# Causal scores of a vision tower on one core: per-slot padding moved from the queries to the keys, with SBUF-to-SBUF DMAs, 392-column products and another order of the queues

## The reference

```python
h = _L0_tok_ref(x, ...)                                 # patches, norm, product, norm
h = h + _L0_attn_ref(_layernorm(h, axis=-1), ...)       # causal attention, 12 heads of 16
h = h + _L0_ffn_ref(_layernorm(h, axis=-1), ...)        # routed attention or mix, then MLP

# in _L0_attn_ref
q = q * scale
scores = jnp.einsum('bhid,bhjd->bhij', q, k)
scores = scores + jnp.einsum('bhid,jd->bhij', q, rel)
scores = jnp.where(causal, scores, -jnp.inf)
probs = jax.nn.softmax(scores, axis=-1)
y = jnp.einsum('bhij,bhjd->bhid', probs, v)
```

## Time and profile before

| | us |
|---|---|
| median of three runs | 7268.11 (7267.75 to 7270.31) |
| the profiled execution, first to last instruction (span) | 7259.2 |
| the profiled execution's own time outside the span | not noted; the median is 8.9 above the span |
| PE busy | 6605.1 |
| PEld busy | 5936.7 |
| DVE busy | 5383.8 |
| ACT busy | 3644.6 |
| POOL busy | 3111.4 |
| mean granted TensorE clock | 0.906 of 2.4 GHz |

### The profile page before, as it was taken

The page is one execution under the profiler, slowest core; times in us unless marked ns, Lnnn a source line. Parts: engine busy times, 40 slices in busy tenths (PEclk is TensorE's granted clock), DMA queues, the critical chain, the costliest instruction groups (busy, mean ns, idle before and its releaser), DMA issues.

```text
span 7259.2 us, 167273 instructions
## 1 busy us (share of the span) xinstructions
PE 6605.1 (91%) x56000; PEld 5936.7 (82%) x56000; DVE 5383.8 (74%) x15934; ACT 3644.6 (50%) x12160; POOL 3111.4 (43%) x4048
## 2 busy tenths in 40 slices
PE   4999999999999999999999999999999999999998
PEld 4888888888888888888888888888888888888887
DVE  3777777777777777777777777777777777777776
ACT  1545555554555455545545554555455455545554
POOL 4444444444444444444444444444444444444443
PEclk8889899999899998989989998999899999899998
DMA  4211121112111111211121111112111211121110
GB/s 46 29 22 23 22 29 22 23 22 29 22 23 26 25 23 22 27 23 23 22 29 22 23 25 25 23 22 28 23 23 22 29 22 23 22 29 22 23 24 8
DMA packets 228657, 175.83 MB, mean 24 GB/s; under 512 B 27785, under 2 KB 228126, under 8 KB 228630
## 3 DMA queue, kind: packets, MB, share of 16 engines
q1 hardware_dynamic: 218934, 173.46, 18.4%
q10 hardware_dynamic: 8336, 1.07, 0.2%
q0 software_dynamic: 1360, 0.96, 0.1%
HBM read 156.11 MB, written 19.27 MB: 24 GB/s over the span
## 4 chain that ended last, share of the span: by engine, by line
issue 34%; PE 20%; DVE 18%; POOL 15%; POOLq 9%; DVEq 3%; ACT 1%; ACTq 0%
PE bank L693 7%; POOL diag L502 6%; DVE qz L1109 5%; POOL rstd L487 4%; PE bank L645 4%; DVE negmax L1128 2%; DVE z L1062 2%; PE bank L681 2%; POOLq L556 2%; POOL h L557 2%; PE bank L781 2%; POOLq L486 2%; POOL res L565 2%; PE bank L792 2%; POOLq L582 2%
## 5 line engine op out<-in xcount | busy, mean ns | idle before, releaser
L1514 ACT ACTIVATE p<-bank,negmax 98x98 f32<-98x98 f32 (+1 forms) x3072 | 1132.3, 376 | 317.6 <-DVE negmax L1128 274.6
L714 PEld LDWEIGHTS bank<-diag,p 128*98 128x98 f32 x9216 | 1066.0, 202 | 157.1 <-issue 104.0
L714 PE MATMUL bank<-diag,p 128*98 128x98 f32 x9216 | 1175.1, 291 | 14.7 <-POOL diag L502 1.7
L1522 ACT COPY pT<-bank 98x392 f32<-98x392 f32 x768 | 374.7, 488 | 1542.2 <-PE bank L714 1542.1
L693 PE MATMUL bank<-tokw,x_sb 128*98 128x193 f32 x4096 | 924.3, 382 | 9.1 <-DVEq L1049 9.1
L502 POOL TENSOR_TENSOR diag<-ident,rden 98x588 f32<-98x588 f32 x512 | 608.4, 1199 | 648.2 <-DVE rden L1142 648.2
L693 PEld LDWEIGHTS bank<-tokw,x_sb 128*98 128x98 f32 x4096 | 825.0, 260 | 67.5 <-issue 29.2
L1128 DVE TENSOR_REDUCE negmax<-bank 98x1 f32<-98x196 f32 (+2 forms) x1536 | 626.1, 456 | 269.0 <-PE bank L681 268.7
L681 PE MATMUL bank<-qk_parts,qz 128*98 128x196 f32 (+1 forms) x6144 | 744.7, 265 | 0.0
L681 PEld LDWEIGHTS bank<-qk_parts,qz 128*98 128x98 f32 x6144 | 656.8, 166 | 11.4
L520 POOL TENSOR_TENSOR qz<-qk_parts,ones 32x588 fp32r<-32x588 f32 x256 | 301.2, 1176 | 721.8 <-DVE qk_parts L1099 701.5
(11 more groups left out here) (272 smaller groups left out, 14889.4 us busy)
## 6 DMA issues: line engine op xcount, KB each, us to landing
x_sb<-in_x SPq DMA_DIRECT2D x384, 196.0 KB, 4.8
x_sb<-in_x SPq DMA_DIRECT2D x384, 189.0 KB, 8.0
out<-out_row SPq DMA_DIRECT2D x128, 147.0 KB
x_store<-in_L_tok_W SPq DMA_DIRECT2D x6, 96.0 KB
diag<-in_L_ffn_W SPq DMA_DIRECT2D x1, 576.0 KB
gstore<-in_L_ffn_W SPq DMA_DIRECT2D x1, 384.0 KB
p<-in_L_attn_w_attn ACTq DMA_DIRECT2D x2, 96.0 KB
gstore<-in_L_ffn_W ACTq DMA_DIRECT2D x1, 192.0 KB
```

Source lines behind the costliest of these rows:

```text
L714: last = mm(bank[b][0:HT, HT * i:HT * i + HT], src, diag[:, h // 3, t, h % 3], start=True, stop=True)
L1514: sc.activation((p1 if t else p0)[0:HT, 3 * s + g], bank[b][0:HT, c0:c0 + (T if t else HT)], ACT.Exp, bias=negmax[:, s, t, g:g + 1], accum ...
L1522: sc.copy(pt_dst(name[0], int(name[1:])), bank[RING[name]][0:HT, 0:4 * HT]).then_inc(sem["pT_act"], 1)
```

## The change

- `wk` leads: k is projected before q, ScalarE copies `khi` and then loads its table and copies `qhi`, VectorE makes `klo` before `qparts`.
- `qz` and its four copies are gone. The queries' parts are used as they are. The keys get a padded tile `kz` of 128 x (2 parts, 4 slots, 3 groups, 196): for each image, SP issues four DMAs of 32 partitions x 2352 bytes for `khi`, and when `klo` is made four for that. They land behind the semaphores `khiz_in` and `kloz_in`, which S0 waits for.
- A score unit is now a group and a tile, nine in all: (g, t = 0) has four slots of 98 columns, (g, t = 1) is two units of two slots of 196. Each is a mask product and two products of 392 columns.
- `maxima` is one reduction in each unit, `inverse_sums` and `diagonals` are three in place of four (eight blocks in place of six).
- Order and banks: S8 after S7 on TensorE, A0 in bank 0, A1 in bank 3 (the embedding's), B0 ahead of A2; on VectorE `maxima(7)` ahead of `max2` and the patch variance, `maxima(3)` ahead of `inverse_sums(0)`; ScalarE copies A3 and VectorE A4.
- Room: `x_store` is gone, and the squares share `gstore`; `p2T` shares the scratch of the ranking; the raw embedding weights lie in `pT0`.

```diff
-RING = dict(S0=0, S1=1, S2=2, T0=3, S3=0, S4=1, S5=2, S6=0, S7=1, A0=2, A1=0, A2=3, B0=1, A3=2,
-            B1=0, A4=1, A5=3, B2=0)
+RING = dict(S0=0, S1=1, S2=2, T0=3, S3=0, S4=1, S5=2, S6=0, S7=1, S8=2, A0=0, A1=3, B0=1, A2=2,
+            A3=0, B1=1, A4=2, A5=3, B2=0)
-PT_ACT = ("A1", "B0", "B1", "A4", "A5", "B2")
+PT_ACT = ("A1", "B0", "A3", "B1", "A5", "B2")
 def s_unit(u):
-    s, second = divmod(u, 2)
-    if second:
-        return s, [(0, 1, 0), (1, 1, T)]
-    return s, [(2, 1, 0), (0, 0, T), (1, 0, T + HT), (2, 0, T + 2 * HT)]
+    g, part = divmod(u, 3)
+    if part:
+        return g, 1, range(2 * part - 2, 2 * part), T
+    return g, 0, range(4), HT
...
+            def place_keys(n):
+
+                for part, made, landed in ((0, "khi_sb", "khiz_in"), (1, "klo_sb", "kloz_in")):
+                    sp.wait_ge(sem[made], after(made, n))
+                    for s in range(4):
+                        at = slice(32 * s, 32 * s + 32)
+                        sp.dma_start(kz[at, part, s].bitcast(F32),
+                                     qk_parts[at, part].bitcast(F32)).then_inc(sem[landed], 16)
...
             with sp.Fori(0, B - 3) as j:
+                place_keys(j + 1)
                 prefetch(j + 2, j + 3)
                 store(j)
...
-                if front:
-
-                    for i in (2, 3):
-                        at = slice(32 * i, 32 * i + 32)
-                        gp.drain()
-                        if i == 2:
-                            gp.wait_ge(sem["qparts_sb"], after("qparts_sb", n))
-                        gp.tensor_tensor(qz[at, i], qparts[at].bitcast(F32),
-                                         ones[at, 0:1].unsqueeze(2).broadcast_to([32, NG, T]),
-                                         ALU.mult).then_inc(sem["qz2_sb"], 1)
-                    gp.drain()
...
+                    group_cols(2, split["wk"], "k_mm")
                     group_cols(0, split["wq"], "q_mm")
-                    group_cols(2, split["wk"], "k_mm")
...
-                    for i, (g, t, c0) in enumerate(heads):
-                        w = T if t else HT
-                        for part in (khi, klo):
-                            last = mm(bank[b][0:HT, c0:c0 + w],
-                                      qz[:, s, g, HT * t:HT * t + HT], part[:, g, 0:w],
-                                      start=False, stop=i == len(heads) - 1 and part is klo,
-                                      skip_group_check=True)
+                    for part in range(2):
+                        last = mm(o, qparts[:, g, HT * t:HT * t + HT],
+                                  kz[:, part, slots[0]:slots[-1] + 1, g, 0:w], start=False,
+                                  stop=part == 1, skip_group_check=True)
...
                 if front:
                     causal("S7")
+                    causal("S8")
                     causal("A0")
                     causal("A1")
                 if back:
                     transposes2()
                 if front:
+                    causal("B0")
                     causal("A2")
-                    causal("B0")
...
                 if front:
+                    keys()
                     query_parts()
-                    slot_queries(0)
-                    slot_queries(1)
-                    keys()
...
                     maxima(6)
                     inverse_sums(1)
+                    maxima(7)
                 if back:
                     max2()
                 if head:
                     patch_variance()
                 if front:
-                    maxima(7)
-                    inverse_sums(2)
+                    maxima(8)
                 if head:
                     embedding()
                 if front:
+                    inverse_sums(2)
                     transposed("A0")
-                    inverse_sums(3)
...
                     mix()
                     attn_out()
                 if front:
-                    transposed("A3")
+                    transposed("A4")
                 if head:
                     h1_stats()
```

More of the change, by code:

```diff
@@ L439, in _ @@
             gp.memset(same_dim, 0.0)
-            gp.memset(qz[:].bitcast(F32), 0.0)
+            gp.memset(kz[:].bitcast(F32), 0.0)
             gp.memset(ones[:], 1.0)
@@ L444, in _ @@
             gp.memset(v_sb[:], 0.0)
-            for t in (pT0, pT1, tokw):
+            for t in (pT1, tokw):
                 gp.memset(t[:], 0.0)
@@ L450, in _ @@
             gp.memset(x_sb[KX:128], 0.0)
+            gp.memset(pT0[KX:128], 0.0)
             gp.drain()
@@ L551, in step @@
                     diagonals(2)
-                    diagonals(3)
                 if head:
@@ L713, in transposes @@
                         src = p1[:, h, HT * u:HT * u + HT] if t else p0[:, h]
-                        last = mm(bank[b][0:HT, HT * i:HT * i + HT], src, diag[:, h // 3, t, h % 3],
+                        last = mm(bank[b][0:HT, HT * i:HT * i + HT], src, diag[:, h // 4, t, h % 4],
                                   start=True, stop=True)
@@ L1123, in maxima @@
                     ve.wait_ge(sem["s_mm"], after("s_mm", n, k + 1))
-                    b, s = RING[f"S{k}"], k // 2
-                    parts = ([(1, 0, 2, 0, T)] if k % 2 else
-                             [(1, 2, 1, 0, T), (0, 0, 3, T, HT)])
-                    for t, g, gn, c0, w in parts:
-                        last = ve.tensor_reduce(
-                            negmax[:, s, t, g:g + gn],
-                            bank[b][0:HT, c0:c0 + w * gn].rearrange("p (h w) -> p h w", w=w),
-                            AX.X, ALU.max, negate=True)
-                    last.then_inc(sem["rowmax"], 1)
+                    g, t, slots, w = s_unit(k)
+                    ve.tensor_reduce(
+                        negmax[:, g, t, slots[0]:slots[-1] + 1],
+                        bank[RING[f"S{k}"]][0:HT, 0:w * len(slots)].rearrange(
+                            "p (s w) -> p s w", w=w),
+                        AX.X, ALU.max, negate=True).then_inc(sem["rowmax"], 1)
                 def transposed(name):
@@ L1377, in step @@
                 if front:
+                    maxima(3)
                     inverse_sums(0)
-                    maxima(3)
                     maxima(4)
@@ L1579, in step @@
                 if front:
+                    keys()
+                    load_table(ACT.Exp)
                     queries()
-                    load_table(ACT.Exp)
-                    keys()
                     values()
@@ L1606, in step @@
                     softmax(7)
+                    softmax(8)
                 if back:
```

103 lines of the change are left out of this document (49 added, 54 removed).

## The result

The kernel after takes **7350.42 us** (median of four runs, 7344.64 to 7355.39), against 7269.04 for the kernel before: a ratio of 1.011, 95% interval 1.0096 to 1.0124. It is slower by 1.1%, where the forecast was 7154 and faster. The time lies in the range (6935 to 7400), the sign is wrong. The profiled execution has a span of 7342.9 us and a mean granted clock of 0.929 (before: 0.906).

The account below looks back on a forecast made before the run. A step was taken as TensorE's in-order work, plus holes from VectorE and GpSimd chains, plus about ten us at 1.2 GHz. Stretch by stretch this gave 54.6 us, 0.9 less over 127 steps: 7154 us, faster, range 6935 to 7400.

Parts of the forecast that it names:

- The whole sum: Whole loop step: 54.6 us forecast, 0.9 less than the mean step of the kernel before.
- rival D: Neither new idle stretch of TensorE costs clock: 52.9 us a step, 6938 us in all; chance 0.13.
- Keys and S0: Step start to first scores: the key DMAs land so that S0 starts at 3613.8, a new hole of 0.9 us.
- Scores: Score products: 0.19 us per 392-column product, 0.46 per late unit, 4.4 us per image, 1.1 less than before.
- Up to the square sums: Gather and first embedding at the full clock: eight token products take 2.86 us, square sums end 3.1 to 3.4 us earlier.
- Rival C: Clock falls after the hole before S0: 1.55 us comes back, 56.1 us a step, 7344 us in all; chance 0.08.
- A1: Before the A1 transposes: tok_y comes 4.5 us after the square sums, not 2.7, so TensorE idles about 2.8 us.
- Mix: Start of TensorE's mix product: 3636.0 against 3637.46, leaving 1.5 of the 3.3 us gained earlier in the step.
- Mix to the end of the scatter: This TensorE stretch runs at the full clock and takes 5.1 us, against 8.3 before, almost all at 1.2 GHz.
- Rival B: A4 evacuation decides, costing 1.3 to 2.3 us; mix-to-scatter stays at 1.2 GHz in half the steps: 56.4 mean, 7382; chance 0.22.
- Scatter to projection: Copying A4 after the scatter makes this 7.3 us against 6.0, plus 0.5 at the low clock after a 2.7 us idle.
- Projection to the next step: Chain through h2 takes 9.25 us; up and down products hide below it with 0.8 to spare, 0.3 lost at low clock.

## Why the forecast failed

**The whole sum.** At the full clock the step after was forecast at 52.9 (rival D) and measured 53.2, with both waits filled. What was wrong is the clock's loss: 1.7 in the forecast (0.9 ahead of the mix, 0.5 and 0.3 behind the wait for `f`), 3.1 measured. 54.6 + 0.3 + 1.4 is 56.3, and 56.25 was measured.

**Where the time of the change went.** The change with both orders as before takes 2.12 off the step at the full clock (51.32 to 49.20). The two waits give 3.97 back (49.20 to 53.17): 2.29 by the A4 evacuation and 1.69 by the place of `maxima(7)`. The clock's loss goes from 4.23 to 3.08. Together -2.12 + 3.97 - 1.15 = +0.70, the measured 55.55 to 56.25. Without the two orders no clock is lost at all, and the change is worth 6.35 us per step, 2.12 of work and waits and 4.23 of clock. How much of that the longer products, the keys first, the query copies that are gone or the one `diagonals` less give was not run.

Step by step, with the times from the token transposes in the step shown:

- **Keys and S0**: right, by two errors that cancel. S0 starts 9.89 after (forecast 9.91). The eight issues took 4.97 us, 0.62 each and not 0.49, and the landing 2.0, not the 3.1 to 3.5 that I allowed.
- **The Trainium skill** ("DMA: Bandwidth & Descriptors", the table of two cost components) gives 2.2 us for such a DMA, as an estimate from its figures. The table stands in the part on DMAs that GpSimd issues, and these are SyncE's; the measured 2.0 (at most 2.7) is near it all the same. What I made of it, that the keys would be there in time, was not so, because of the issues: S0 waited 0.95 us.
- **Scores**: right. Late units start 0.44 to 0.48 us apart, mask and two products of 392 columns in each (forecast 0.46).
- **Up to the square sums**: right. The clock stays up over the first embedding, its sixteen instructions take 2.93 us (2.86), and the square sums end 22.9 after (22.7). Rival C is out.
- **A1**: size right, cause half right. `tok_y` comes 4.3 us after the square sums (4.5), TensorE is idle for 2.71 (2.8). The place of `maxima(7)` makes 1.7 of it and bank 3 nothing; 1.0 is left in either bank.
- **Mix**: 32.8 after, in the step shown and in the mean of 115 steps, against 32.1. This is the first mis-sized term, and the smaller one. I charged 0.9 for low clock behind A1 on a floor of 31.2. The transposes of the attention and of the routed block run at 0.50 for 3.4 us here, and with both waits filled the mix comes at 31.5: the low clock costs 1.3.
- **Mix to the end of the scatter**: right, 5.0 us at 1.00 (5.1). Rival B gave 56.4 us per step, near the measured 56.25, but by the old clock in this stretch. It has its price of the A4 evacuation right (2.29, at the upper end of its 1.3 to 2.3) and its main mechanism wrong.
- **Scatter to projection**: right, 7.8 (7.3 and 0.5).
- **Projection to the next step**: the second mis-sized term and the larger one, 10.9 in the mean and 11.5 in the step shown, forecast 9.55. I wrote that up and down products hide below the chain through `h2` with 0.8 to spare, and 0.3 are lost at the low clock. At 1.2 GHz that cover is gone: the stretch is 9.4 with both waits filled, so the low clock costs 1.5. With both orders undone TensorE is through with the up product 4.87 us after the projection's start, and it waits 0.79 for `z`; in the kernel after that takes 7.10 us. Then the GELU parts come late on VectorE, and `z` is queued behind the third of them. The first group is TensorE with both orders undone, the second VectorE in the kernel after:

```profile
3199.96 1.29 PE L869 MATMUL bank<-wps,qk_parts 128*98 128x192 f32 x12
3201.23 3.60 PE L636 MATMUL bank<-nTs,w_split 128*128 128x196 f32 x30
...
3209.36 0.56 PE L620 MATMUL bank<-ident,z 98*128 98x98 f32 x4 [0.79 <-DVE z L1055]
```

```profile
3803.55 1.20 DVE L1319 TENSOR_TENSOR qk_parts<-gstore,qk_parts 128x392 fp32r<-128x392 f32 x1
3804.68 0.66 DVE L1055 TENSOR_SCALAR z<-h,mv_f,vf 98x192 f32<-98x192 f32 x2
```

- **The stretches together**: to the mix, from there to the projection, and from there to the next step, the means are 32.8, 12.5 and 10.9, the forecast was 32.1, 12.9 and 9.55. That is 0.7, -0.4 and 1.3, which makes 54.6 into 56.2.

The error behind both terms is one. I had seen 0.61 and 0.50 behind waits of 1.0 and 1.8 us, and priced the low clock behind two waits of 2.7 us at 1.7 in all. The old waits cost 4.23 together, the new ones 3.08.

The Trainium skill ("TensorE: Matmul & The Clock Gate", "HAM oscillation — how this bites in real kernels") describes a kernel that waits, falls to the low clock and starts each round at half speed, and prices the loss at half the time spent low. This case agrees in kind and comes out somewhat lower in size: 7.51 us of low clock would be 3.75 by that price, and 3.08 came back when both waits were filled; in the kernel before 9.94 us cost 4.23.

## What to carry to other kernels

Price a new wait of TensorE at its length plus the low clock behind it. Take the price from what the waits of the kernel before cost, which filling them with spare products measures (a price per us of waiting did not come out of these runs), and ask which cover further down the low clock takes away. Before an operation is moved ahead on an in-order engine, look at what it waits for and who waits for those behind it: a maxima of 0.57 us, moved ahead of two short steps, cost 3.9 us per step, and VectorE's evacuation of A4 in place of A3 4.7. A large loss can hide a good change: with these two orders set back the same change is 11.3% faster than before.

## What the runs showed of the hardware that was not expected

- Work that fills a wait can pay for itself. 28 added mask products, about 5 us of TensorE per step, made the step 3.1 us shorter, and 10 ahead of the mix in the kernel before 3.9 shorter.
- The loss is not additive over waits. Idle stretches of 0.94 and 1.04 us in one step (both orders undone) went with a clock of 1.00 in all 115 steps, and the one of 0.96 in the kernel before did in 91 of 115 once the other was filled.
- A microsecond of low clock cost 0.41 to 0.43 us of the step in these kernels (3.08 for 7.51 and 4.23 for 9.94), not half. Why less was not shown.
- A DMA of 75 KB inside SBUF, in rows of 2352 bytes, lands 2.0 us after its issue, and one of twice the bytes in 2.7 (medians). The issue takes SP 0.59 us, so that eight in a row are slower than four larger ones that start later, by 0.6 us a step (56.25 to 55.66).
